# Cross attention and FFN on one core: query norms folded into the exponential's scale

## The reference

```python
x = x + xattn(layernorm(x), ctx, Wq, Wk, Wv, Wo, gq, gk)
x = x + ffn(layernorm(x), W_fc, W_proj)

# xattn: x is (4, 256, 256), ctx (4, 256, 128), 16 heads of width 128
q = rmsnorm((h @ Wq).reshape(B, Sq, H, D), gq)      # x * rsqrt(mean(x^2) + 1e-5) * g
k = rmsnorm((c @ Wk).reshape(B, Skv, H, D), gk)
v = (c @ Wv).reshape(B, Skv, H, D)
attn = softmax(einsum('bqhd,bkhd->bhqk', q, k) / sqrt(D))
out = einsum('bhqk,bkhd->bqhd', attn, v).reshape(B, Sq, H * D) @ Wo

# ffn: both weights are made ternary in groups of 64
h = square(relu(x @ w1.T)); h = h * rsqrt(mean(h^2) + eps); out = h @ w2.T
```

## Time and profile before

| | |
|---|---|
| time, median of 3 executions | 333.14 us (333.05 to 333.31) |
| the profiled execution | 333.5 us, its span 331.3 us |
| PE busy | 319.6 us, 96% of the span |
| DVE busy | 270.1 us, 82% |
| ACT busy | 268.4 us, 81% |
| POOL busy | 211.4 us, 64% |
| granted TensorE clock | 1.0 of full speed throughout |

### The profile page before, as it was taken

The page is one execution under the profiler, slowest core; times in us unless marked ns, Lnnn a source line. Parts: engine busy times, 40 slices in busy tenths (PEclk is TensorE's granted clock), DMA queues, the critical chain, the costliest instruction groups (busy, mean ns, idle before and its releaser), DMA issues.

```text
span 331.3 us, 8010 instructions
## 1 busy us (share of the span) xinstructions
PE 319.6 (96%) x2597; PEld 310.4 (94%) x2597; DVE 270.1 (82%) x567; ACT 268.4 (81%) x1054; POOL 211.4 (64%) x306
## 2 busy tenths in 40 slices
PE   7799999999999999999999999999999999998994
PEld 6698899999999999999999999999999998896983
DVE  3567688977889878888898788888987878779965
ACT  3788788888888888888888888888888888686761
POOL 4686789848886685666666856666668562235652
PEclk9999999999999999999999999999999999999999
DMA  6972415000000000000000000000000000000003
GB/s 185 365 229 79 130 48 176 3 0 3 0 2 4 0 2 0 4 0 3 3 0 2 1 2 2 2 2 0 3 3 0 3 1 2 0 2 0 3 0 127
DMA packets 10553, 11.51 MB, mean 35 GB/s; under 512 B 785, under 2 KB 10001, under 8 KB 10513
## 3 DMA queue, kind: packets, MB, share of 16 engines
q1 hardware_dynamic: 10080, 10.88, 10.2%
q10 hardware_dynamic: 432, 0.13, 0.2%
HBM read 9.96 MB, written 1.05 MB: 33 GB/s over the span
## 4 chain that ended last, share of the span: by engine, by line
PE 84%; DVE 5%; issue 3%; ACT 2%; POOL 2%; DMA 2%; SPq 1%; POOLq 0%; ACTq 0%; DVEq 0%
PE bT L806 8%; PE bO L714 5%; PE bS L714 5%; PE bY L714 5%; PE bA L714 4%; PE bA L716 4%; PE bO L716 4%; PE bA L715 4%; PE bO L715 4%; PE bY L716 4%; PE bY L715 4%; PE bS L715 4%; PE bS L716 4%; PE bT L783 4%; PE bT L772 4%
## 5 line engine op out<-in xcount | busy, mean ns | idle before, releaser
L419 POOL TENSOR_SCALAR Pr<-Pr,rs 128x256 f32<-128x256 f32 x128 | 65.6, 526 | 52.0 <-DVE rs L1121 46.3
L569 ACT ACTIVATE Pr<-bS,nb 128x256 f32<-128x256 f32 x128 | 59.3, 474 | 0.0
L414 POOL TENSOR_TENSOR rr<-sse,mhalf 128x8 f32<-128x8 f32 x30 | 50.0, 1667 | 2.5
L577 ACT ACTIVATE PTh<-bT 128x512 fp32r<-128x512 f32 x64 | 39.6, 618 | 11.2 <-PE bT L806 11.2
L1114 DVE TENSOR_REDUCE nb<-bS 128x2 f32<-128x512 f32 x64 | 44.1, 689 | 5.5 <-PE bS L716 2.0
L1075 DVE TENSOR_TENSOR PTl<-bT,PTh 128x512 fp32r<-128x512 f32 x64 | 43.5, 680 | 0.6 <-ACT PTh L577 0.5
L583 ACT ACTIVATE Oh<-bO 128x256 fp32r<-128x256 f32 x64 | 25.5, 399 | 21.7 <-PE bO L716 21.6
L714 PE MATMUL bY<-WWh,Oh 128*128 128x256 f32 x128 | 41.3, 323 | 0.0
L1075 DVE TENSOR_TENSOR Ol<-bO,Oh 128x256 fp32r<-128x256 f32 x64 | 26.8, 419 | 17.0 <-ACT Oh L583 16.9
L714 PE MATMUL bO<-PTh,ch 128*128 128x256 f32 x128 | 39.0, 305 | 0.2
L806 PE MATMUL bT<-ident,Pr 128*128 128x128 f32 x256 | 38.4, 272 | 0.0
(11 more groups left out here) (209 smaller groups left out, 1138.0 us busy)
## 6 DMA issues: line engine op xcount, KB each, us to landing
Wqr<-in_L_xattn_Wq SPq DMA_DIRECT2D x8, 256.0 KB, 4.3
Wor<-in_L_xattn_Wo SPq DMA_DIRECT2D x2, 1024.0 KB, 10.0
Wkr<-in_L_xattn_Wk SPq DMA_DIRECT2D x8, 128.0 KB, 3.0
Wvr<-in_L_xattn_Wv SPq DMA_DIRECT2D x2, 512.0 KB, 7.5
WvT<-in_L_ffn_W_fc SPq DMA_DIRECT2D x1, 1024.0 KB, 5.6
Wor<-in_L_ffn_W_proj SPq DMA_DIRECT2D x1, 1024.0 KB, 6.3
xt<-in_x SPq DMA_DIRECT2D x1, 768.0 KB, 11.6
out<-xn SPq DMA_DIRECT2D x3, 256.0 KB, 2.1
```

Source lines behind the costliest of these rows:

```text
L414: gp.tensor_tensor(rr[:, :], sse[:, :], mhalf[:, 0:2 * UT], ALU.pow).then_inc(r_done, 1)
L419: last = gp.tensor_scalar(Pr[u][:, t, :], Pr[u][:, t, :], rs[u][:, t:t + 1], 1.0, ALU.mult, ALU.mult)
L569: last = act.activation(Pr[u][:, t, :], bS[u][:, t * SKV:(t + 1) * SKV], ACT.Exp, bias=nb[u][:, t:t + 1], scale=1.0, accum_out=su[u][:, t: ...
L577: act.activation(PTh[u][:, :, :].rearrange(flat3), bT[u][:, :], ACT.Copy).then_inc(pth_done[u], 1)
```

## The change

- `q_norm` is gone. `q_copy` copies the raw queries from `bA` to `qn`, waiting only for PE; the queries are turned and multiplied without their norm.
- The norm of a query is a factor of its whole row of scores, so it is now the `scale` operand of the exponential, one number per partition. The largest score has to be multiplied by it too: `maxes` writes `mx`, and a new multiplication of 128 x 2 numbers makes `nb = mx * rr`, after a wait for `mx` itself and for `rr`. There are 64 of these.
- `square_q` reads the copy `qn` in SBUF instead of the PSUM bank. In the loop it stands between the two `exps`, for pair i + 2, instead of at the end of the step for pair i + 3.
- POOL computes the norms of keys and of queries apart (`key_norms`, `query_norms`) in two halves of `rr`, of which there are now two in turn.
- At the start, queries are copied and turned before the keys, and the four `wv_copy` on ACT stand behind `q_hi` and `k_hi`.
- At the end, the last two tiles of the output leave in one transfer on SP instead of one on SP and one on ACT.

```diff
-            def norms(n):
-                gp.wait_ge(sqk_done, n + 1)
-                gp.wait_ge(sqq_done, n + 1)
-                gp.tensor_scalar(sse[:, :], ss[:, :], EPS * D, None, ALU.add).then_inc(sse_done, 1)
...
-                gp.tensor_tensor(rr[:, :], sse[:, :], mhalf[:, 0:2 * UT], ALU.pow).then_inc(r_done, 1)
...
                 if pair(i + 2) and i >= 0:
-                    norms(i + 2)
+                    key_norms(i + 2)
...
+                if pair(i + 2) and i >= 4:
+                    query_norms(i + 2)
...
+                if pair(i + 2) and 0 <= i < 4:
+                    query_norms(i + 2)
...
             def square_q(n):
-                act.wait_ge(q_done, n + 1)
+                act.wait_ge(qn_done, n + 1)
...
-                    last = act.activation(sqj[:, j, :], bA[:, j * D:(j + 1) * D], ACT.Square,
+                    last = act.activation(sqj[:, j, :], qn[:, j, :], ACT.Square,
...
                     last = act.activation(Pr[u][:, t, :], bS[u][:, t * SKV:(t + 1) * SKV], ACT.Exp,
-                                          bias=nb[u][:, t:t + 1], scale=1.0, accum_out=su[u][:, t:t + 1])
+                                          bias=nb[u][:, t:t + 1], scale=rr[n % 2][:, 2 * t + u:2 * t + u + 1],
+                                          accum_out=su[u][:, t:t + 1])
...
             turn_wv(1)
+            turn_q(0)
             turn_k(0)
             pe.wait_ge(s_wv[1], 16)
             turn_wv(2)
             turn_wv(3)
-            turn_q(0)
...
-            def q_norm(n):
-                dve.wait_ge(r_done, n + 1)
+            def q_copy(n):
+                dve.wait_ge(q_done, n + 1)
                 if n >= 1:
                     dve.wait_ge(qt_done, n)
-                dve.tensor_tensor(qn[:, :, :], bA[:, :].rearrange("p (t d) -> p t d", t=UT),
-                                  rr[:, 0:UT].unsqueeze(2).broadcast_to([P, UT, D]), ALU.mult).then_inc(qn_done, 1)
+                    dve.wait_ge(sqq_done, n)
+                dve.tensor_copy(qn[:, :, :].rearrange(flat3), bA[:, :]).then_inc(qn_done, 1)
...
             def maxes(n, u):
                 dve.wait_ge(s_done[u], n + 1)
-                dve.tensor_reduce(nb[u][:, :], bS[u][:, :].rearrange("p (t k) -> p t k", t=QT), AX.X,
-                                  ALU.max, negate=True).then_inc(nb_done[u], 1)
+                dve.tensor_reduce(mx[u][:, :], bS[u][:, :].rearrange("p (t k) -> p t k", t=QT), AX.X,
+                                  ALU.max, negate=True).then_inc(mx_done[u], 1)
+                dve.wait_ge(r_done, n + 1)
+                dve.wait_ge(mx_done[u], n + 1)
+                dve.tensor_tensor(nb[u][:, :], mx[u][:, :],
+                                  rr[n % 2][:, 0:UT].rearrange("p (t u) -> p t u", u=2)[:, :, u],
+                                  ALU.mult).then_inc(nb_done[u], 1)
```

More of the change, by code:

```diff
@@ L105, in xattn_ffn @@
         sse = sb("sse", [P, 2 * UT])
-        rr = sb("rr", [P, 2 * UT])
+        rr = [sb(f"rr{i}", [P, 2 * UT]) for i in range(2)]
         qn = sb("qn", [P, UT, D])
@@ L112, in xattn_ffn @@
         kl = sb("kl", [P, 2, SKV], f32r)
+        mx = [sb(f"mx{u}", [P, QT]) for u in range(2)]
         nb = [sb(f"nb{u}", [P, QT]) for u in range(2)]
@@ L218, in xattn_ffn @@
         s_done = [sem("s_done0"), sem("s_done1")]
+        mx_done = [sem("mx_done0"), sem("mx_done1")]
         nb_done = [sem("nb_done0"), sem("nb_done1")]
@@ L358, in _ @@
             sp.wait_ge(yo_done, T4 // 2 + 2)
-            sp.dma_start(out_v[:, T4 + 2, :], yo[:, T4 + 2, :]).then_inc(s_out, 16)
-            sp.wait_ge(s_out, 16 * (T4 // 2 + 3))
+            sp.wait_ge(yo_pool, 1)
+            sp.dma_start(out_v[:, T4 + 2:NT, :], yo[:, T4 + 2:NT, :]).then_inc(s_out, 16)
+            sp.wait_ge(s_out, 16 * (T4 // 2 + 2))
         @block.gpsimd
@@ L441, in key_norms @@
                 gp.wait_ge(ssek_done, n + 1)
-                if n >= 1:
-                    gp.wait_ge(kn_done, n)
-                gp.tensor_tensor(rr[:, UT:2 * UT], sse[:, UT:2 * UT], mhalf[:, 0:UT], ALU.pow).then_inc(rk_done, 1)
+                if n >= 2:
+                    gp.wait_ge(kn_done, n - 1)
+                gp.tensor_tensor(rr[n % 2][:, UT:2 * UT], sse[:, UT:2 * UT], mhalf[:, 0:UT], ALU.pow).then_inc(rk_done, 1)
             def query_norms(n):
@@ L449, in query_norms @@
                 gp.wait_ge(sse_done, n + 1)
-                if n >= 1:
-                    gp.wait_ge(qn_done, n)
-                gp.tensor_tensor(rr[:, 0:UT], sse[:, 0:UT], mhalf[:, 0:UT], ALU.pow).then_inc(r_done, 1)
+                if n >= 2:
+                    for u in range(2):
+                        gp.wait_ge(exp_done[u], n - 1)
+                gp.tensor_tensor(rr[n % 2][:, 0:UT], sse[:, 0:UT], mhalf[:, 0:UT], ALU.pow).then_inc(r_done, 1)
             split_k_hi(0)
@@ L638, in _ @@
             square_q(0)
-            wv_copy(0)
+            q_hi(0)
             act.wait_ge(s_gg, 1)
             k_hi(0)
-            wv_copy(1)
-            wv_copy(2)
-            wv_copy(3)
-            q_hi(0)
+            for n in range(H // 4):
+                wv_copy(n)
             square_q(1)
@@ L668, in _ @@
                     exps(i + 1, 0)
+                if pair(i + 2) and i >= 0:
+                    square_q(i + 2)
                 if i == 0:
@@ L686, in _ @@
                     ww_hi(7)
-                if pair(i + 3):
-                    square_q(i + 3)
                 if i == STEPS - 3:
@@ L1194, in finish_first, with split_q1 @@
                 finish_tile(0, 2 * half + 1).then_inc(yo_done, 1)
+            def split_q1():
+                dve.wait_ge(s_wq[1], 16)
+                dve.tensor_copy(Wqh[1], Wqr[1][:, :, :]).then_inc(wqh1_done, 1)
+                dve.wait_ge(wqh1_done, 1)
+                dve.tensor_tensor(Wql[1], Wqr[1][:, :, :], Wqh[1].bitcast(f32), ALU.subtract).then_inc(wql1_done, 1)
             dve.wait_ge(s_x[0], 16)
@@ L1203, in _ @@
             x_lo(1)
+            q_copy(0)
             ctx_lo(1, bS[1][:, :])
@@ L1206, in _ @@
             k_norm(0)
-            dve.wait_ge(s_wq[1], 16)
-            dve.tensor_copy(Wqh[1], Wqr[1][:, :, :]).then_inc(wqh1_done, 1)
-            dve.wait_ge(wqh1_done, 1)
-            dve.tensor_tensor(Wql[1], Wqr[1][:, :, :], Wqh[1].bitcast(f32), ALU.subtract).then_inc(wql1_done, 1)
-            q_norm(0)
+            split_q1()
+            q_lo(0)
             k_lo(0)
-            q_lo(0)
+            q_copy(1)
             for i in range(-1, STEPS):
@@ L1229, in _ @@
                     ww_lo(5)
-                if pair(i + 2):
-                    q_norm(i + 2)
+                if pair(i + 2) and i >= 0:
+                    q_copy(i + 2)
                 if i > 0 and i % PAIRS == 0:
```

15 lines of the change are left out of this document (3 added, 12 removed).

## The result

The changed kernel takes 343.42 us (median of 4 runs, 343.24 to 343.78) against 333.23 before (4 runs, 333.05 to 333.87): a ratio of 1.0298, 95% interval 1.0286 to 1.0311, 10.2 us slower. The profiled execution is the longest of the four, 343.78 us, with a span of 341.7.

A forecast was written before the change was run, and what follows sets the result against it. PE, busy 96% of the span, was taken to bound the kernel, with DVE taking over in dense steps. Terms 3.2 + 0.4 + 0.9 + 1.0 + 0.6 - 0.5 - 0.4 = +5.2 gave a 338.3 us median, range 333.0 to 341.8.

The forecast's parts named there:

- DVE's ring: Chain from maximum to next maximum, nearly all DVE work: 7.93 us before, 8.47 with the products, over PE's 8.20.
- dense steps: Twelve steps with t_compare and t_scale (6, 7, 11 to 15, 19 to 23): +0.27 us each, +3.2 in all.
- all terms for it together: The product's cost over dense steps, residual steps, steps 3, 4 and 29, and light steps: 6.1 us.
- Rival 1: The wait between maximum and product is free, so no dense step is late: 332.4 us, chance 0.12.
- Rival 2: The query copy on DVE is a fast one, 0.42 us: 333.3 us, no change, chance 0.07.
- The three late `kh` of the context steps: In steps 6, 11 and 19 kh on ACT is no longer late: 3 x 0.17, -0.5 us.
- the term on ACT: Squares fill idle time before Oh, late kh disappear, -0.5 us; longer exponentials are hidden, nothing taken for them.
- Rival 3: ACT is not hidden: exponentials run 0.09 us longer each and rs waits for them; 340 to 342 us, chance 0.13.
- 9, 17 and 25: Where the cost of residual steps 8, 16 and 24 shows: DVE's 8.94 against 8.64 us, +0.9 in all.
- 3, 4 and 29: Step 3 has a layer norm, +0.4 us; in 4 and 29 PE already waits for DVE, +1.0.
- the light ones: Eleven steps (1, 2, 5, 9, 10, 17, 18, 25 to 28): PTl arrives on the edge, +0.6 us.
- the start: PE's wait for the norm before the first turned queries shrinks, keys come later: -0.4 us, bounds -2.0 and +0.5.

The follow-up runs named there:

- e1: Kernel before with only a product by ones added right behind each maximum, with its two waits: 341.04 us.
- e9: Kernel before with the exponentials taking their scale, one, from a column of ones, no product: 333.94 us.
- e10: Kernel before with both the product by ones and the exponentials' scale from a column of ones: 341.56 us.
- e2: Changed kernel without the product; the bias is the bare maximum and the exponentials wait for the norms themselves: 337.11 us.
- e16: Changed kernel with only the products moved away from their maxima, behind PTl and behind kn: 348.70 us.
- e5: Changed kernel with the query squares moved behind the same step's second exponentials and the query norms last on POOL: 343.65 us.
- e14: Changed kernel with squares back at their old place from pair 2 on and query norms right behind key norms: 341.54 us.
- e11: Changed kernel with only the squares back at their old place; stalled early on POOL's late query norms: 354.40 us.
- e3: Changed kernel with the constant 0.09 as the exponentials' scale instead of the query norms, product kept: 342.35 us.
- e6: Changed kernel without maxima and products, the exponentials' bias set to 0: 331.90 us.

## Why the forecast was right in direction and half in size

*Right: the product and DVE's ring.* `nb` starts 0.79 to 0.80 behind `mx`, and a maximum with its product takes 0.87 to 0.89 (forecast 0.88). With the product alone (e1) the dense steps are 8.43 to 8.47 and all terms for it together are +6.0 for 6.1, apart from what steps 12 and 23 lose. Rival 1 did not happen. The Trainium skill ("VectorE: DVE Perf Modes", section "The DRAIN you can't avoid") has it, of copies with a semaphore behind each, that the semaphore costs nothing extra. For an operation that waits for the one right ahead of it the runs decide otherwise: here 64 products right behind their reductions cost 7.7 us, and the same 64 with the same waits, moved 0.60 us on, cost none that could be measured (333.24 us). Rival 2 did not happen either: the copy takes 0.68. The second operand costs 0.09 us a time and is hidden in the dense steps of the kernel before (e9, e10). The Trainium skill ("ScalarE: Activation LUTs", section "What ACT_TABLE_LOAD costs") gives about 93 ns for each pointer operand; the trace agrees for a second one, 474 to 562 ns. The three late `kh` of the context steps did go: 0.33 us together, 0.5 forecast. The end changed nothing.

*Wrong: the squares in the term on ACT.* It said that they "now fill the stretch in front of `Oh` where ACT was idle, 21.7 us in 64 waits". 64 is the number of `Oh` instructions; the view of waits of the kernel before (us in total, times, longest) has 33 waits:

```profile
ACT Oh L583 <- PE bO L716: 21.6, 33, 1.1
```

So the stretch comes once a step and is 0.65 us long (21.6 / 33); four squares take 1.18. They do not fit, push `Oh` and everything behind it by half a microsecond, and close a ring through both engines at 8.65, over DVE's 8.47. In the trace of the changed kernel ACT is never idle on it. Without a product (e2) the step is 8.47 all the same, where DVE alone would have kept under 8.2. Starting the first exponentials 0.40 later (e16) lengthened the step by 0.29 and the whole by 5.3 us, though no product held DVE up any more. Taking the squares out from between the exponentials brought the dense steps to 8.49 (e5) and 8.48 (e14), each time with the query norms moved too, and to 8.57 with the squares alone (e11); e14 is 1.9 us shorter in all.

The same term took nothing for the second operand, as hidden. That holds beside the old place of the squares (0.5 us, e10), not in the ring that they close: there a constant scale gave back 1.1 us (e3). Rival 3 had this symptom, `rs` waiting for `Pr`. But it had only the longer exponentials for a cause, and its 340 to 342 was too low.

Set against the forecast by the differences of step lengths in the two traces (10.4 us up to step 31, for 5.2): the twelve steps behind dense ones +5.7 for 3.2, since a plain one is 8.64 to 8.76 and not 8.47; 9, 17 and 25 +1.2 for 0.9; 3, 4 and 29 +1.7 for 1.4; the light ones +1.2 for 0.6. Of this, 0.22 each is in 10, 18 and 26, whose predecessors hold a layer norm's statistics of 1.16 us (10 and 26 are 8.22 to 8.23 in e1, 18 is 8.53), and 0.32 in 28, where a product lasts 0.45 until POOL's `wpos` ends. Steps 6, 11 and 19 gave back 0.33 for 0.5. The start holds the other 0.9.

*Wrong, but not by a known amount: the start.* A gain of 0.4 was forecast, and step 2 begins 0.9 us late in the trace. Of this, 0.7 is there when step 0 begins, where the traces of one and the same start differ by 1.5 us (e2 0.3 early, e6 1.2 late). What repeats in all of them is that the squares for pair 2, ahead of `WWh`, make step 0 0.9 to 1.1 us longer and step 1 0.85 to 0.95 shorter; in the changed kernel the two together are 0.24 longer. I had named that they push `WWh`, and gave it no price. The new order of the first pairs is neither a loss nor the gain that was forecast: undone, it left the time where it was (343.45).

*What stays open.* Outside the dense steps it was not tried how the 1.9 us of e14 divide between the squares and the query norms. Why step 23 of e1 has its `gsr` late, and why step 18 is 8.53 there, is not explained. What the start costs would need several traces of each kernel.

## What to carry to other kernels

When work is moved into idle time, compare the length of one idle stretch with the length of the work, not their sums, and then follow the chain that passes through the place, over both engines. A small operation on a reduction's result is cheap only if something else stands between the two; but what reads its result then starts later, and in this kernel the same move was worth 7.8 us in one schedule (341.04 to 333.24) and cost 5.3 in another. A ring is not found by adding distances from start to start, which give the step along any path. Add what each instruction needs by itself, as the forecast did for DVE: where this falls short of the step (8.47 of 8.65), look for the instruction in it that waits, and follow what it waits for into the other engine until nothing on the path is idle.
